# Moving the score-maximum matmuls next to the value matmuls, and normalising queries and keys two token tiles at a time, in a hand-scheduled language-model layer

## The chip, the cores and the metric

The kernel runs on one core of one Trainium2 chip. The metric is the device time of one launch in microseconds, as the median of several runs. The core has five engines that run side by side and meet at semaphores: TensorE (PE in the profile; PEld is its loading of the stationary operand), VectorE (DVE), ScalarE (ACT), GpSimd (POOL) and SyncE (SP), which issues most of the DMA transfers. Each engine takes its own instructions strictly in the order in which the program lists them, and an instruction that waits holds up all that stand behind it on its engine.

## What is computed

`x` holds 2 rows of 2048 token numbers. Each is looked up in an embedding table (50257 entries of width 256), and then one attention layer and one mixture-of-experts layer are added to the residual `h`:

```python
h = take(table, tokens) + bias                     # 2 x 2048 x 256
h = h + attention(layernorm(h))                    # 16 heads of 64, causal
h = h + experts(layernorm(h))                      # top 2 of 8 experts, and a shared one
# attention: xn = layernorm(x) * g + b
q = l2norm(xn @ Wq) * q_scale;  k = l2norm(x @ Wk) * k_scale;  v = x @ Wv   # 2 null keys and values ahead
sim = 8 * q @ k.T - slope * distance;  attn = softmax(causal(sim));  out = (attn @ v) @ Wout
```

The two lines on `q` and `k` are what the change rewrites: each token's 64 numbers per head are divided by their length, and the keys are also multiplied by a vector of 64 scales (`scl` holds `q_scale * k_scale * 8`).

## The kernel before

Two heads are worked on at a time, called a pair: 8 pairs for each of the 2 rows of tokens, 16 pairs `t` in all. The 2048 tokens are 16 tiles of 128 (`T`), and 4 tiles are a group of query columns `ig` (512 wide).

For a pair the work has four stages.

**Projection** (`project`). For each of 17 token tiles `s` PE makes q, k and v of that tile (`proj`, L1400 and L1403). ACT squares q and k (`square`, L875), copies v and copies q and k to `tqk` (L879). DVE sums the squares (`ssq_`, L1083), POOL takes the inverse root with two small instructions (`inv_norm`, L768 and L771), and DVE multiplies (`unit`): one instruction for q (L1094) and one for each of two heads for k (L1096). For every two tiles, a group `g`, ACT and DVE split the result into a high and a low fp16 half in `blk` (`high`, L886; `low_`, L1103), PE transposes them (`turn`, L1415), ACT keeps them (L898) and SP copies parts of them to the tensor `low` (`copy_low`).

**Row maxima** (`maxima`). The softmax subtracts each query's maximum. 44 units per pair (`scores_a`, L1431) are a first, coarser scores matmul for both heads at once: a 64*128 stationary operand in each half of the array. DVE reduces each head's result to a maximum (`max_`, L1123, with a small instruction that reads the result out). The two banks that `scores_a` writes are single: the next `scores_a` waits on PE until both reductions of the one before are done (`a_read`).

**Attention** (`attend`). The keys run down in 44 steps of two blocks (one block of each head; 88 blocks `m` per pair). PE makes the scores (`scores`, L1458 and L1459, on the diagonal also a mask, L1462; stationary operand 128*128), ACT takes the exponential (`exp`, L919) into one of six buffers `probs`, PE multiplies with v (`values`, L1474; stationary operand 128*64, both heads in one pass), and POOL, for one of the eight column groups DVE, adds up the row sums (`sum_p`, L790 and L1161).

**Output**. PE sums over the partitions (`sums`, L1484), ACT copies to `rl`, SP turns the sums by DMA through a column (`turn_l`), DVE inverts (`inv_l`), SP spreads them again by DMA (`spread_l`), DVE divides (`divide`, L1173), PE multiplies with Wout (`wout`, L1494), and DVE adds to `h` (`add_o`, L1181).

At last come the gate and the experts (`gate`, `routed`, `shared_expert`), which the change hardly touches.

All of it is interleaved by a plan written out by hand. `at(time, kind, ...)` gives every piece a due time; the unit of time is one block of `attend`, so that a pair takes 88 units. The plan is sorted, and each engine issues its part of every piece in that order. The due times set an order only; nothing waits for a time. While pair `t` is attended, the projection of pair `t + 1` and its maxima run in between. `turn_of` keeps pieces that use one of the two shared banks a certain distance apart. For a pair that begins at `t0`:

```python
at(t0 + m - 0.9 * (m % 2), "scores", t, m)           # 0, 0.1, 2, 2.1, 4, ...
at(t0 + (m | 1) + 3.5, "values", t, m)               # 4.5, 4.5, 6.5, 6.5, ...
s0 = max(s0 + step, halves[(t, ...)])                # scores_a: from t0 - 35 in steps of 1.85
project(t, t0 + PAIR * t - 74.0, 5.0)                # a token tile every 5 units
```

## Time and profile before

| | us |
|---|---|
| median of 3 runs | 2745.8 (2736.39 to 2750.08) |
| the profiled execution, its own time | 2751.77 |
| its span, first to last instruction | 2750.0 |
| PE busy | 2424.1 (88%) |
| DVE busy | 2027.2 (74%) |
| POOL busy | 1594.1 (58%) |
| ACT busy | 1406.6 (51%) |

Shares of busy time are averages over stages. In the profile, a row of a group gives busy time, the mean duration of one instruction, and the idle time of its engine just before instructions of that group with what ended it. A matmul's duration holds its way through the array; two that follow each other start closer together than one lasts, so the distance between starts in the timeline is the time that one costs PE. `64*128 64x512` is a stationary operand of 64 rows and 128 columns with a moving one of 512 columns. The first pair is attended from 114 us on, the sixteenth pair's last scores stand at 2433 us, and the rest is the experts.

### The profile page before, as it was taken

Reading aid. Unit: us, or ns where it says so; the run is one execution under the profiler, and the core shown is the slowest. Engines: PE = TensorE matmul, PEld = TensorE weight load, DVE = VectorE, ACT = ScalarE, POOL = GpSimd, SP = SyncE. Lnnn points to the kernel's source line nnn. Section 1 sums busy time; section 2 is a strip of 40 time slices with the busy share of each in tenths; the row PEclk is TensorE's granted clock in tenths of the full one; section 3 lists DMA queues with packets and bytes.
Section 4 is the critical chain, followed back from the end, with each engine's and each line's share of the span. In section 5 each row is a group of like instructions: output and inputs, shape, how many; then the busy total and the mean of one; then the engine's idle time right before and its main releaser. Section 6 shows DMA issues by size and latency. Waiting matters only on the chain.

```text
span 2750.0 us, 49117 instructions
## 1 busy us (share of the span) xinstructions
PE 2424.1 (88%) x13353; PEld 1204.6 (44%) x13353; DVE 2027.2 (74%) x5748; ACT 1406.6 (51%) x3094; POOL 1594.1 (58%) x1901
## 2 busy tenths in 40 slices
PE   2789999999989988898999999999999997877887
PEld 2434344444434434343444444444434443446775
DVE  6678787878777878878787878787878786644444
ACT  3445455655554646565555555554646563324541
POOL 6365656666675656575757575656565665462424
PEclk8899999999999999999999999999999998868999
DMA  2000111011111011011111000001000002023543
GB/s 46 18 19 19 34 25 37 24 36 26 30 45 23 24 25 31 20 34 28 34 28 30 17 22 15 25 16 25 16 25 15 21 15 82 9 86 112 163 128 123
DMA packets 155702, 106.65 MB, mean 39 GB/s; under 512 B 63728, under 2 KB 139632, under 8 KB 155440
## 3 DMA queue, kind: packets, MB, share of 16 engines
q1 hardware_dynamic: 147760, 82.52, 11.6%
q0 software_dynamic: 7680, 20.98, 2.5%
q8 instruction: 122, 2.00, 0.3%
q14 instruction: 140, 1.15, 0.2%
HBM read 52.94 MB, written 33.29 MB: 31 GB/s over the span
## 4 chain that ended last, share of the span: by engine, by line
PE 29%; DVE 10%; DMA 6%; issue 5%; POOL 2%; SPq 2%; ACT 2%; another core or an unknown queue 1%; ACTq 0%; DVEq 0%; POOLq 0%
PE ps L1474 5%; PE ps L1458 3%; DVE ps L1123 3%; PE ps L1459 3%; DMA rl<-l_row 3%; PE ps L1555 2%; PE ps L1431 2%; PE ps L1541 2%; PE ps L1403 2%; DMA l_row<-l_col 2%; PE ps L1494 1%; PE ps L1400 1%; DVE acc L1161 1%; DVE tqk L1096 1%; PE ps L1484 1%
## 5 line engine op out<-in xcount | busy, mean ns | idle before, releaser
L790 POOL TENSOR_TENSOR acc<-acc,probs 128x512 f32<-128x512 f32 (+4 forms) x944 | 911.5, 966 | 200.3 <-ACT probs L919 114.8
L919 ACT ACTIVATE probs<-ps,btab 128x512 f32<-128x512 f32 (+4 forms) x1408 | 775.5, 589 | 445.8 <-PE ps L1459 282.8
L1123 DVE CUSTOM_DVE_ANT_0 ps<-ps,tab_l 128x512 f32<-128x512 f32 (+1 forms) x896 | 565.9, 671 | 172.4 <-PE ps L1431 170.3
L1474 PE MATMUL ps<-probs,arena 128*64 128x512 f32 (+4 forms) x2816 | 642.7, 534 | 0.0
L1458 PE MATMUL ps<-arena 128*128 128x512 f16 (+4 forms) x1408 | 482.8, 343 | 23.1 <-ACT probs L919 10.6
L1459 PE MATMUL ps<-arena 128*128 128x512 f16 (+9 forms) x1408 | 479.6, 341 | 0.0
L1431 PE MATMUL ps<-arena 64*128 64x512 f16 (+4 forms) x1408 | 247.2, 344 | 120.1 <-DVE mx L1123 115.3
L768 POOL TENSOR_SCALAR nsq<-ssq 128x4 f32<-128x4 f32 (+1 forms) x272 | 62.0, 228 | 475.3 <-DVE ssq L1083 474.2
L771 POOL TENSOR_TENSOR rnorm<-nsq,minus_half 128x4 f32<-128x4 f32 (+1 forms) x272 | 282.6, 1039 | 22.6
L1403 PE MATMUL ps<-wqkv,xT 128*128 128x256 f32 (+1 forms) x1088 | 287.4, 388 | 0.0
L1431 PEld LDWEIGHTS ps<-arena 64*128 64x128 f16 x1408 | 74.9, 93 | 464.1 <-issue 454.4
L1458 PEld LDWEIGHTS ps<-arena 128*128 128x128 f16 (+1 forms) x1408 | 137.2, 97 | 272.5 <-issue 129.4
L1096 DVE SCALAR_TENSOR_TENSOR tqk<-tqk,rnorm,scl 128x64 f32<-128x64 f32 (+1 forms) x544 | 247.8, 494 | 0.0
L1123 DVE CUSTOM_DVE_ANT_0 ps<-ps,tab_r 128x258 f32<-128x258 f32 (+2 forms) x512 | 207.2, 445 | 51.2 <-PE ps L1431 49.4
L1094 DVE TENSOR_TENSOR tqk<-tqk,rnorm 128x128 f32<-128x128 f32 x256 | 184.9, 722 | 69.4 <-POOL rnorm L771 67.9
L1474 PEld LDWEIGHTS ps<-probs,arena 128*64 128x64 f32 (+1 forms) x2816 | 142.5, 138 | 197.9 <-issue 118.8
L875 ACT ACTIVATE sq<-ps 128x256 f32<-128x256 f32 (+1 forms) x272 | 101.6, 373 | 241.6 <-PE ps L1403 241.6
L886 ACT ACTIVATE blk<-tqk 128x512 f16<-128x512 f32 x128 | 80.7, 630 | 281.0 <-DVE tqk L1096 281.0
L1494 PE MATMUL ps<-wo,otf 128*128 128x256 f32 x512 | 177.2, 429 | 42.6 <-DVE otf L1173 41.0
L1123 DVE DVE_READ_ACCUMULATOR2_ANT mx<- 128x1 f32 x1408 | 194.2, 138 | 0.0
L1403 PEld LDWEIGHTS ps<-wqkv,xT 128*128 128x128 f32 (+1 forms) x1088 | 183.9, 189 | 22.0 <-issue 2.2
L1400 PE MATMUL ps<-wqkv,xnT 128*128 128x128 f32 x1024 | 178.2, 298 | 4.8 <-ACT xnT L865 4.8
(176 smaller groups left out, 3350.5 us busy)
## 6 DMA issues: line engine op xcount, KB each, us to landing
arena<-arena SPq DMA_DIRECT2D x512, 32.0 KB, 1.9
rl<-l_row SPq DMA_DIRECT2D x128, 128.0 KB
x_rows<-arena SPq DMA_DIRECT2D x78, 128.0 KB, 2.2
arena<-x_rows SPq DMA_DIRECT2D x78, 128.0 KB
...
```

The costliest lines, as they stand in the source:

```text
L771: pool.tensor_tensor(rnorm[0:rows, s % 2, c0:4], nsq[0:rows, s % 2, c0:4], minus_half[0:rows, c0:4], ALU.pow).then_inc(rnorm_ready, 1)
L790: pool.tensor_tensor(a, probs[0:rows, (n - 2) % PB, 0:GW] if first else a, p, ALU.add).then_inc(sum_pool, 1)
L919: nc.scalar.activation(probs[0:rows, n % PB, 0:w], bank(S0 + n % 2)[0:rows, 0:w], ACT.Exp, bias=btab[0:rows, hh, z:z + 1]).then_inc(exp_do ...
L1096: last = nc.vector.scalar_tensor_tensor(out=k[:, hd, :], in0=k[:, hd, :], scalar=rnorm[0:rows, s % 2, 2 + hd:3 + hd], in1=scl[0:rows, :], ...
L1123: nc.vector.tensor_tensor_reduce(bank(A0 + hd)[:, 0:w], bank(A0 + hd)[:, 0:w], tab, 1.0, NEG, ALU.add, ALU.max, mx[:, hd, it, c:c + 1]).th ...
L1400: mm(o[:, 0:128], xnT[:, c, 128 * s:128 * s + 128], wqkv[:, r, c, 0:128], start=(c == 0), stop=(c == C - 1))
L1403: last = mm(o[0:rows, 128:384], xT[:, c, 128 * s:128 * s + rows], wqkv[:, r, c, 128:384], start=(c == 0), stop=(c == C - 1))
L1431: mm(bank(A0 + i)[:, 0:w], l[half, 0, i, 128 * it:128 * it + 128], l[half, 1, i, k0:k0 + w], start=True, stop=True).then_inc(a_ready, 1)
L1458: mm(dst[0:rows, 0:w], s[:, 1, hd, j], s[:, 0, hd, q], start=True, stop=False)
L1459: last = mm(dst[0:rows, 0:w], l[SPAN[hd], 1, hd, j], l[SPAN[hd], 0, hd, q], start=False, stop=not diag)
L1474: mm(bank(O0 + o % 2)[DH * hd:DH * hd + DH, c0:GW], vt[t % 2][0:rows, jt, hd, :], probs[0:rows, n % PB, 0:GW - c0], start=(jt == 0), stop= ...
L1494: mm(bank(z)[:, 0:D], otf[:, o % 2, 128 * k:128 * k + 128], wo[:, r, :], start=True, stop=True).then_inc(w_ready, 1)
```

## The change

It has three parts.

1. **The order on PE.** `scores_a` is given due times on a grid: always 1.88 units after an even block, with its steps of 1.92 rounded up to the next place of that grid. `values` is due at 1.95 of the same two units instead of 0.5, so that `scores_a` stands straight ahead of `values`, and `values` straight ahead of the next two blocks of scores. The reduction `max` is due together with its `scores_a`.
2. **Norms and unit vectors for two tiles at once.** `ssq`, `inv_norm` and `unit` run once for a group `g` of two tiles (9 times per pair instead of 17). `ssq` sums 8 rows of 64 (a 128x512 input) and is followed by a new multiplication of the keys with `scl` (128x256), which needs no norm; `unit` is one multiplication of q and k of both tiles with the inverse norms (128x512) in place of six. `sq` has one buffer of 512 instead of two of 256, so that the squares of a new group wait for `ssq` of the group before. `tqk` and `blk` are numbered on through the pairs.
3. **Places in a pair.** The projection starts at 77.5 instead of 74 units ahead of its pair and the maxima at 42 instead of 35. `values`, `sum_p`, `exp` and `sums` have new lags; `divide` is due 9.1 instead of 6.1 units after `sums`, `wout` 11.4 instead of 7.7; the distances of `turn_of`, and the places of the embedding of the second row and of its gate, move too.

The diff, cut to its core:

```diff
-        apart = 0.65 if time < 0 else 0.9
+        apart = 0.7 if time < 0 else 1.05
...
-    LAGS = [dict(square=0.4, ssq=1.2, inv=1.9, unit=3.2, high=3.5, low=4.3, turn=4.8),
-            dict(square=0.9, ssq=2.0, inv=2.3, unit=4.2, high=5.0, low=5.8, turn=7.0)]
+    LAGS = [dict(square=0.3, ssq=1.05, inv=1.6, unit=2.0, high=3.3, low=4.1, turn=5.55),
+            dict(square=1.0, ssq=1.6, inv=2.8, unit=4.2, high=5.0, low=5.5, turn=7.0)]
...
-            s0 = max(s0 + step, halves[(t, (units[n][0] + 1) // 2)])
+            due = max(due + step, halves[(t, (units[n][0] + 1) // 2)])
+
+            s0 = t0 + 2 * math.ceil((due - t0 - 1.88) / 2) + 1.88 if t > 0 else due
             at(s0, "scores_a", t, n)
-            at(s0 + 0.6, "max", t, n)
+            at(s0 + 0.0, "max", t, n)
...
-                s1 = turn_of(s0 + 5.5)
+                s1 = turn_of(s0 + 4.5)
                 at(s1, "turn_shift", t, ig)
...
-            at(t0 + m - 0.9 * (m % 2) + 0.5, "exp", t, m)
-            at(t0 + m - 0.9 * (m % 2) + 1.85, "sum_p", t, m)
-            at(t0 + (m | 1) + 3.5, "values", t, m)
+            at(t0 + m - 0.9 * (m % 2) + 0.8, "exp", t, m)
+            at(t0 + m - 0.9 * (m % 2) + 2.6, "sum_p", t, m)
+            at(t0 + (m | 1) + 2.95, "values", t, m)
...
-            at(s0 + 6.1, "divide", t, ig)
+            at(s0 + 9.1, "divide", t, ig)
...
-                w0 = turn_of(max(sums_at[(t, ig)] + 7.7, wout_from[0] + 2.4))
+                w0 = turn_of(max(sums_at[(t, ig)] + 11.4, wout_from[0] + 2.4))
...
-    project(0, -24, 1.7)
-    maxima(0, -14.4, 1.2)
+    project(0, -24, 1.25)
+    maxima(0, -14.4, 1.3)
...
-        project(t, t0 + PAIR * t - 74.0, 5.0)
+        project(t, t0 + PAIR * t - 77.5, 5.0)
     for t in range(1, PAIRS):
-        maxima(t, t0 + PAIR * t - 35.0, 1.85)
+        maxima(t, t0 + PAIR * t - 42.0, 1.92)
...
-                need(act, ssq_ready, n - 1)
-                nc.scalar.activation(sq[0:rows, s % 2, c0:256], p[0:rows, c0:256], ACT.Square).then_inc(sq_ready, 1)
+                need(act, ssq_ready, PG * t + s // 2)
+                nc.scalar.activation(sq[0:rows, :].rearrange("p (z u n) -> p z u n", z=2, u=2)[:, c0 // 128:2, s % 2, :],
+                                     p[0:rows, c0:256].rearrange("p (z n) -> p z n", n=128), ACT.Square).then_inc(sq_ready, 1)
...
+                dve.wait_ge(sq_ready, done)
                 need(dve, nsq_ready, n - 1)
-                nc.vector.tensor_reduce(ssq[0:rows, s % 2, c0:4], sq[0:rows, s % 2, 64 * c0:256].rearrange("p (a d) -> p a d", d=DH),
+                nc.vector.tensor_reduce(ssq[0:rows, (PG * t + g) % 2, cs], sq[0:rows, DH * cs.start:DH * cs.stop].rearrange("p (a d) -> p a d", d=DH),
                                         AX.X, ALU.add).then_inc(ssq_ready, 1)
...
+                k = tqk[0:rows, (PG * t + g) % 2, 256:DH * cs.stop].rearrange("p (a d) -> p a d", d=DH)
+                dve.wait_ge(p_read, done)
+                nc.vector.tensor_tensor(k, k, scl[0:rows, :].unsqueeze(1).to_broadcast([rows, cs.stop - 4, DH]), ALU.mult).then_inc(k_scaled, 1)
...
-                if s < T:
-                    nc.vector.tensor_tensor(q, q, rnorm[0:rows, s % 2, 0:2].unsqueeze(2).to_broadcast([rows, 2, DH]), ALU.mult)
-                for hd in range(2):
-                    last = nc.vector.scalar_tensor_tensor(out=k[:, hd, :], in0=k[:, hd, :], scalar=rnorm[0:rows, s % 2, 2 + hd:3 + hd],
-                                                          in1=scl[0:rows, :], op0=ALU.mult, op1=ALU.mult)
-                last.then_inc(qk_read, 1)
+                dve.wait_ge(k_scaled, n + 1)
+                qk = tqk[0:rows, (PG * t + g) % 2, DH * cs.start:DH * cs.stop].rearrange("p (a d) -> p a d", d=DH)
+                nc.vector.tensor_tensor(qk, qk, rnorm[0:rows, (PG * t + g) % 2, cs].unsqueeze(2).to_broadcast([rows, cs.stop - cs.start, DH]),
+                                        ALU.mult).then_inc(qk_read, 1)
```

The order of PE in the middle of a pair before, rows in a row. L1458 and L1459 are the scores (`arena` holds their operands), L1474 is `values`, L1431 `scores_a`, L1494 `wout`, L1400 and L1403 a projection:

```order
L1474 MATMUL ps<-probs,arena 64x512 x2
L1400 MATMUL ps<-wqkv,xnT 128x128 x2
L1403 MATMUL ps<-wqkv,xT 128x256 x2
L1431 MATMUL ps<-arena 128x512 x2
L1494 MATMUL ps<-wo,otf 128x256
L1458 MATMUL ps<-arena 128x512
L1459 MATMUL ps<-arena 128x512
L1458 MATMUL ps<-arena 128x512
L1459 MATMUL ps<-arena 128x512
L1474 MATMUL ps<-probs,arena 64x512 x2
L1431 MATMUL ps<-arena 128x512 x2
L1458 MATMUL ps<-arena 128x512
```

The order of PE in the change near the same place of a pair; its lines stand 5 further down (L1463 and L1464 scores, L1479 `values`, L1436 `scores_a`, L1499 `wout`, L1405 and L1408 a projection):

```order
L1479 MATMUL ps<-probs,arena 64x512 x2
L1463 MATMUL ps<-arena 128x512
L1464 MATMUL ps<-arena 128x512
L1463 MATMUL ps<-arena 128x512
L1464 MATMUL ps<-arena 128x512
L1405 MATMUL ps<-wqkv,xnT 128x128 x2
L1408 MATMUL ps<-wqkv,xT 128x256 x2
L1436 MATMUL ps<-arena 128x258 x2
L1479 MATMUL ps<-probs,arena 64x512 x2
L1463 MATMUL ps<-arena 128x512
```

`scores_a` no longer stands alone among 128*128 operands; it is followed by `values`. Counted over the whole program, PE changes from one size of the stationary operand to another 2718 times before and 2559 times after, and the number of `scores_a` (704) that have neither `values` nor `sums` for a neighbour falls from 212 to 58.

The order of PE in the change further on in the same pair, among the diagonal blocks (L1467 is the mask):

```order
L1463 MATMUL ps<-arena 128x258
L1464 MATMUL ps<-arena 128x258
L1467 MATMUL ps<-mask_b,ident 128x128
L1436 MATMUL ps<-arena 128x258 x2
L1436 MATMUL ps<-arena 128x386 x2
L1479 MATMUL ps<-probs,arena 64x386 x2
```

Two `scores_a` fall on one place of the grid and follow each other directly, with nothing between them. This happens 28 times in pairs 2 to 15; before, no two stood side by side there.

The order of DVE in the middle of a pair before. L1123 is `max` (shown as ISA, with its read-out), L1173 `divide`, L1083 `ssq`, L1094 and L1096 `unit`:

```order
L1083 TENSOR_REDUCE ssq<-sq 128x4
L1173 TENSOR_TENSOR otf<-ps,rl 128x512
L1123 ISA ps,mx<-ps,tab_l 128x512
L1123 ISA mx 128x1
L1123 ISA ps,mx<-ps,tab_l 128x512
L1123 ISA mx 128x1
L1094 TENSOR_TENSOR tqk<-tqk,rnorm 128x128
L1096 SCALAR_TENSOR_TENSOR tqk<-tqk,rnorm,scl 128x64 x2
```

The order of DVE in the change at a like place (L1128 `max`, L1178 `divide`, L1090 and L1094 `ssq` and the scaling of the keys, L1102 `unit`, L1186 `add_o`):

```order
L1090 TENSOR_REDUCE ssq<-sq 128x8
L1094 TENSOR_TENSOR tqk<-tqk,scl 128x256
L1186 TENSOR_TENSOR h<-ps,h 128x256
L1128 ISA ps,mx<-ps,tab_l 128x256
L1128 ISA mx 128x1
L1128 ISA ps,mx<-ps,tab_l 128x256
L1128 ISA mx 128x1
L1178 TENSOR_TENSOR otf<-ps,rl 128x512
L1102 TENSOR_TENSOR tqk<-tqk,rnorm 128x512
```

Three wide instructions (L1090, L1094, L1102) stand for a group of two tiles, where eight stood before (L1083, L1094 and twice L1096 for each tile).

## Rows read from the trace of the kernel before

**Rows 1.** The windows view: us, busy us (instructions) of PE, PEld, DVE, ACT, POOL, PEclk.

```profile
268.00:2270.00 2002.00, 1846.91 (x10289) 833.34 (x10286) 1592.20 (x4447) 1109.53 (x2429) 1237.16 (x1450) 0.97 0.11 26
0.00:114.00 114.00, 52.94 (x253) 38.29 (x254) 71.75 (x227) 42.00 (x113) 60.78 (x111) 0.84 0.15 35
```

**Rows 2.** Waits of PE alone, 268 to 2270 us: us in total, times, longest.

```profile
PE ps L1431 <- DVE mx L1123: 84.1, 152, 2.2
PE ps L1494 <- DVE otf L1173: 35.9, 27, 2.8
PE ps L1458 <- ACT probs L919: 10.2, 14, 0.8
PE ps L1458 <- DMA arena<-augs: 6.7, 13, 1.2
PE ps L1415 <- DVE blk L1103: 6.5, 16, 1.8
```

**Rows 3.** Timeline of PE, 1300 to 1326 us: start, length, instruction, idle before it.

```profile
1308.95 0.38 PE L1458 MATMUL ps<-arena 128*128 128x512 f16 x1
1309.17 0.38 PE L1459 MATMUL ps<-arena 128*128 128x512 f16 x1
...
1310.62 0.39 PE L1431 MATMUL ps<-arena 64*128 64x512 f16 x2
1310.94 0.71 PE L1400 MATMUL ps<-wqkv,xnT 128*128 128x128 f32 x4
...
1323.38 1.08 PE L1474 MATMUL ps<-probs,arena 128*64 128x512 f32 x4
1324.39 0.23 PE L1458 MATMUL ps<-arena 128*128 128x130 f16 x1
...
1324.58 0.66 PE L1400 MATMUL ps<-wqkv,xnT 128*128 128x128 f32 x4
```

**Rows 4.** Groups of DVE by shape: busy us, mean ns | idle before, and its end.

```profile
L1123 DVE CUSTOM_DVE_ANT_0 ps<-ps,tab_l 128x512 f32<-128x512 f32 x768 | 514.7, 710 | 168.4 <-PE ps L1431 166.9
L1096 DVE SCALAR_TENSOR_TENSOR tqk<-tqk,rnorm,scl 128x64 f32<-128x64 f32 x512 | 240.4, 508 | 0.0
...
L1094 DVE TENSOR_TENSOR tqk<-tqk,rnorm 128x128 f32<-128x128 f32 x256 | 184.9, 722 | 69.4 <-POOL rnorm L771 67.9
...
L1103 DVE TENSOR_TENSOR blk<-tqk,blk 128x512 f16<-128x512 f32 x128 | 117.5, 918 | 3.2 <-ACT blk L886 3.2
...
L1123 DVE CUSTOM_DVE_ANT_0 ps<-ps,tab_r 128x258 f32<-128x258 f32 x256 | 103.9, 447 | 35.9 <-PE ps L1431 35.9
L1083 DVE TENSOR_REDUCE ssq<-sq 128x4 f32<-128x256 f32 x256 | 103.7, 405 | 7.2 <-ACT sq L875 7.2
```

**Rows 5.** Single lines of DVE: shortest/median/longest ns.

```profile
L1094 DVE TENSOR_TENSOR tqk<-tqk,rnorm x256: 271/590/1406, 50.7 to 2277.8; 128x128 f32<-128x128 f32 x128
...
L1103 DVE TENSOR_TENSOR blk<-tqk,blk x128: 633/749/1675, 65.7 to 2292.9; 128x512 f16<-128x512 f32 x128
```

**Rows 6.** Groups of POOL by shape.

```profile
L771 POOL TENSOR_TENSOR rnorm<-nsq,minus_half 128x4 f32<-128x4 f32 x256 | 271.4, 1060 | 21.3
...
L768 POOL TENSOR_SCALAR nsq<-ssq 128x4 f32<-128x4 f32 x256 | 58.6, 229 | 460.3 <-DVE ssq L1083 459.3
...
L762 POOL TENSOR_TENSOR rstd<-var,minus_half 128x2 f32<-128x2 f32 x48 | 36.6, 763 | 4.0
```

**Rows 7.** Waits of DVE in the whole span: us in total, times, longest.

```profile
DVE otf L1173 <- DMA rl<-l_row: 104.5, 48, 4.3
DVE tqk L1094 <- POOL rnorm L771: 67.9, 62, 4.0
```

**Rows 8.** Timeline of PE, one `scores_a`.

```profile
1334.26 0.39 PE L1431 MATMUL ps<-arena 64*128 64x512 f16 x2
```

**Rows 9.** Timeline of DVE, its second reduction and the read-out.

```profile
1335.30 0.73 DVE L1123 CUSTOM_DVE_ANT_0 ps<-ps,tab_l 128x512 f32<-128x512 f32 x1
1335.95 0.14 DVE L1123 DVE_READ_ACCUMULATOR2_ANT mx<- 128x1 f32 x1
```

More of the change, by code:

```diff
@@ L1 @@
+import math
 import concourse.bass as bass
@@ L140, in project @@
             at(s0 + lag["square"], "square", t, s)
-            at(s0 + lag["ssq"], "ssq", t, s)
-            at(s0 + lag["inv"], "inv_norm", t, s)
-            at(s0 + lag["unit"], "unit", t, s)
             if s == 0:
@@ L147, in project @@
                 g = s // 2
+                at(s0 + lag["ssq"], "ssq", t, g)
+                at(s0 + lag["inv"], "inv_norm", t, g)
+                at(s0 + lag["unit"], "unit", t, g)
                 at(s0 + lag["high"], "high", t, g)
@@ L363, in lm_tower_kernel @@
         rstd = sb("rstd", [128, 3, NB, T])
-        minus_half = sb("minus_half", [128, 4])
+        minus_half = sb("minus_half", [128, 8])
         wqkv = sb("wqkv", [128, 2, C, 3 * 128])
         wo = sb("wo", [128, 2, D])
-        sq = sb("sq", [128, 2, 256])
-        ssq = sb("ssq", [128, 2, 4])
-        nsq = sb("nsq", [128, 2, 4])
-        rnorm = sb("rnorm", [128, 2, 4])
+        sq = sb("sq", [128, 512])
+        ssq = sb("ssq", [128, 2, 8])
+        nsq = sb("nsq", [128, 2, 8])
+        rnorm = sb("rnorm", [128, 2, 8])
         tqk = sb("tqk", [128, 2, 512])
@@ L762, in root, with inv_norm @@
                 pool.tensor_tensor(rstd[:, k, b, us], var[:, k, b, us], minus_half[:, 0:2], ALU.pow).then_inc(rstd_ready[k], 1)
-            def inv_norm(t, s):
-                n = TK * t + s
-                rows, c0 = (128, 0) if s < T else (NN, 2)
+            def inv_norm(t, g):
+                n = PG * t + g
+                rows, cs = (128, slice(0, 8)) if g < PG - 1 else (NN, slice(4, 6))
                 pool.wait_ge(ssq_ready, n + 1)
-                pool.tensor_scalar(nsq[0:rows, s % 2, c0:4], ssq[0:rows, s % 2, c0:4], 1e-24, None, ALU.max).then_inc(nsq_ready, 1)
+                pool.tensor_scalar(nsq[0:rows, (PG * t + g) % 2, cs], ssq[0:rows, (PG * t + g) % 2, cs], 1e-24, None, ALU.max).then_inc(nsq_ready, 1)
                 pool.wait_ge(nsq_ready, n + 1)
                 need(pool, qk_read, n - 1)
-                pool.tensor_tensor(rnorm[0:rows, s % 2, c0:4], nsq[0:rows, s % 2, c0:4], minus_half[0:rows, c0:4], ALU.pow).then_inc(rnorm_ready, 1)
+                pool.tensor_tensor(rnorm[0:rows, (PG * t + g) % 2, cs], nsq[0:rows, (PG * t + g) % 2, cs], minus_half[0:rows, cs], ALU.pow).then_inc(rnorm_ready, 1)
             def sum_p(t, m):
```

80 lines of the change are left out of this document (39 added, 41 removed).

## The prediction

> **What bounds the kernel now.** I read the windows view first. Between 268 and 2270 us, 14 of the 16 pairs, PE is busy 1847 of 2002 us at a granted clock of 0.97, DVE 1592, POOL 1237, ACT 1110 [rows 1]. PE sets the pace, about 143 us a pair, and there are two ways to be faster: less time of PE itself, and less of the 155 us that it idles there. The waits of PE say what the idle time is [rows 2]: 84 us are `scores_a` waiting for the reductions of the one before, 36 us are `wout` waiting for `divide`, and three waits of 6 to 10 us each are scores behind an exponential, scores behind the DMA of the maxima, and the transposes behind `low_`. The clock is near its upper level (2.4 GHz) here, so it has little to give.
>
> **The change, part by part**, against the profiled execution's 2751.8 us; the median of the runs is 6 us below that.
>
> *Changes of the stationary size.* Two scores matmuls of 512 columns start 0.22 us apart; `scores_a`, also 512 columns, is followed by the projection's 128*128 operand after 0.32 us [rows 3]. So a change from one size to another costs PE 0.10 us. 159 fewer of them (2718 to 2559 by the order) are 159 x 0.10 = **-15 us**. It is small because half of the `scores_a` already had a neighbour of values before. Ends: 10 and 20 us less.
>
> *Wout.* It moves from 7.7 to 11.4 units behind `sums`, 3.7 units or some 6 us at 143 / 88 = 1.6 us a unit, and `divide` 3 units. The longest of its waits was 2.8 us [rows 2]. All 36 us should go: **-36**, ends -42 and -25. What is late next is the write to `h`, for which nobody waits within a pair.
>
> *The DMA of the maxima.* The maxima begin 7 units earlier, but step 1.92 instead of 1.85 over 43 steps gives 3 back; the last ones come 4 units earlier, over 6 us, against waits of 1.2 us: **-7**.
>
> *The grid for scores_a.* The banks of `scores_a` come free only after both reductions. From its start at 1334.26 [rows 8] to the end of the second read-out at 1336.09 [rows 9] there are 1.83 us at 512 columns; at 258 columns each reduction is 710 - 447 = 0.26 us shorter [rows 4], so 1.30 us. Where two `scores_a` follow each other directly, the first being 258 wide and 0.2 us long each time, PE must stand for 1.1 us: 28 x 1.1 = +31. Also, in each pair there are three places on the diagonal with nothing but `values` and narrow scores between two `scores_a`. The widest has values of 1.01 us and scores of 0.19 us a block [rows 3] with more columns; by such rows they take 1.7, 1.5 and 1.3 us, which is 0.1 + 0.3 + 0.5 short of 1.83: 14 pairs x 1 = +14. Together **+45**, ends +25 (where DVE would have been late anyway) and +55.
>
> *Norms of two tiles at once, on DVE.* Before, two tiles cost 2 x 0.405 (L1083) + 2 x 0.722 (L1094) + 4 x 0.508 (L1096) = 4.29 us [rows 4]. No row shows the new shapes. The shortest L1094 took 0.271 us for 128 elements and the shortest L1103 0.633 for 512 [rows 5], so 256 elements take about 0.39 at best. Over their shortest, L1094 lost on average 722 - 271 = 0.45 us and L1103 918 - 633 = 0.29 [rows 4, 5]: the loss is one per instruction and doesn't grow with width. So I take 0.39 + 0.3 for the scaling of k, 0.92 for `unit` (as L1103), and 0.405 + 0.26 for the reduction over 512 (a reduction's slope by the 258 and 512 rows, [rows 4]): 2.28 us. 128 groups x 2.0 us = 257 us less on DVE, 13% of its 2027. If the loss grew with width instead, as from 0.45 at 128 elements to 0.9 and 1.8, the three would cost 4.4 us and nothing would be saved. The mean of L1103 speaks against that. The Trainium skill (SBUF — State Buffer, "SBUF: two separate sides") says that DVE instructions with two inputs in SBUF and GpSimd instructions take one port pair by turns, each for its whole length, and whoever comes second waits; by that a delay is paid per meeting, the rows agree, and the sum stays with the per-instruction price. By the same rule wider DVE instructions hold GpSimd off for longer at a time, though for less in all.
>
> DVE is not on PE's path by its sum but by its order: what stands ahead of a reduction makes it late. There are 257 us less of that, and the waits that stood ahead of reductions, 104.5 us of `divide` for its DMA and 67.9 us of `unit` for POOL [rows 7], are due 3 units later and once instead of twice a group. `max` is also due together with its `scores_a`. Of the 84 us of lateness I take seven tenths away: **-60**, ends 0 and -84.
>
> *POOL.* Two tiles cost 2 x (0.229 + 1.060) = 2.58 us. The power takes 0.763 for 2 elements and 1.060 for 4 [rows 6], 0.15 each, so 1.65 for 8, with 0.23 ahead: 1.88 us, 0.7 less per group, 89 us in all. POOL isn't waited for by ACT to speak of, so: 0. But the answer to one `ssq` now comes 0.6 us later, and a `sum_p` may stand ahead; if that cover goes, `unit` waits (rival C).
>
> *ACT, SP.* The instructions of ACT are the same in number and size, and those of SP too; SP's queue passes the same DMAs, `turn_l` earlier and the parts of `low` at the pace of the projection. The squares have one buffer, and ACT waits for `ssq` of the last group, due 3 units before the next tile: 0. The small waits for exponential and transposes, 10.2 + 6.5 us [rows 2], have less in front: **-10**, ends 0 and -17.
>
> *First pair and tail.* Until 114 us PE is busy 53 us and DVE 72 [rows 1]; there the projection is on the path, and 8 groups x 2 us of DVE go, of which I count half: **-8**, ends 0 and -16. The tail keeps its work: 0.
>
> Sum: -15 - 36 - 7 + 45 - 60 - 10 - 8 = -91, or 2751.8 - 91 = 2661 on the profiled execution and **2655** as a median.
>
> **The rivals.**
>
> *A, the stalls go altogether.* If all 84 us of lateness, the small waits and the upper half of the startup go, and the direct neighbours overlap with lateness that was there anyway (+25), the sum is -20 - 42 - 7 + 25 - 84 - 17 - 16 = -161: 2585. For it: DVE has only 1592 of 2002 us to do now. Against it: the 28 neighbours can't be hidden in the order itself.
>
> *B, DVE isn't relieved*, because the wide instructions lose more per instruction than the narrow ones or meet POOL each time; lateness stays and the waits only change place: -15 - 36 - 7 + 45 = -13 to, with a third of the lateness gone and the small terms, -30: 2725. For it: new shapes have no row. Against it: L1103 and L1094 as above.
>
> *C, slower: `unit` waits for POOL ahead of the reductions.* The plan gives `unit` 1.4 units (2.3 us) after `inv_norm`, of which the power now takes 1.88. One `sum_p` in front (over 1 us) makes DVE stand, and the reduction behind it, `scores_a`, `values` and the next scores, which now stand behind each other on PE, stand too. It already waited 67.9 us in 62 cases [rows 7]. If each of 128 groups held PE for 0.5 us, with no lateness removed, and `wout` gained as forecast, the sum is -15 - 36 - 7 + 45 + 64 = +51: 2797. It decides from 0.1 us a group on if nothing else is gained. Against it: 89 us less on POOL, and half as many such waits.
>
> *D, the change isn't in effect on the chip.* The order shows the pieces moved; it could only be that 0.10 us for a change of size is hidden elsewhere. That is 15 us and within the range.
>
> **How the numbers follow.** The forecast has 0.55, A 0.17, B 0.18, C 0.10. The range leaves out C and the part of A below 2570: 2570 to 2735, and takes in the ends of lateness in both directions. A measurement of this kernel can tell about 0.5% (14 us) from no change. Faster by more: the forecast, A, and over half of B, 0.82; within: the rest of B, 0.08; slower: C, 0.10.
>
> **What would show it.** PE's waits in the same 14 pairs: `wout` on `divide` near 0 (else the Wout step is wrong); `scores_a` on `max` 45 + 24 = 70 us, of which 28 waits of about 1.1 us; if over 130, DVE was not relieved. DVE's three new groups at 0.67, 0.69 and 0.92 us in the mean and a busy time of about 1770 us; B if the two multiplications together are over 2.5 us. POOL's power at 1.65 us. C would show as `unit` waiting over 130 us for `rnorm`. A pair should take 137 us instead of 143. Wrong above all: a wait for the exponential or for POOL's sums in place of those for DVE.

## The result, and the profile after

The change takes 2636.0 us as a median of 4 runs (2633.92 to 2640.77), the kernel before in the same comparison 2747.9 us (2736.39 to 2750.51): a ratio of 0.9603, 95% interval [0.9572, 0.9634]. The forecast was 2655, range 2570 to 2735.

The profiled execution of the change. First the page: span, busy time of each engine, and of the 40 slices the rows of PE, DVE and the granted clock:

```profile
span 2633.1 us, 47837 instructions
PE 2370.3 (90%) x13353; PEld 1210.4 (46%) x13353; DVE 1816.8 (69%) x5108; ACT 1419.1 (54%) x3094; POOL 1558.9 (59%) x1645
PE   3789999999999999899999999999999998867897
DVE  6668686767776788768686868686868686634445
PEclk9799999999999999899999999999999998868999
```

The windows view: the same 14 pairs as in [rows 1] (columns as there), then the start and the experts:

```profile
259.00:2160.00 1901.00, 1802.53 (x10285) 840.47 (x10283) 1395.10 (x3885) 1121.38 (x2428) 1206.13 (x1224) 0.98 0.12 27
0.00:119.00 119.00, 56.98 (x294) 41.60 (x295) 77.46 (x222) 47.77 (x127) 62.05 (x103) 0.90 0.15 35
2309.00:2633.00 324.00, 255.70 (x1418) 211.30 (x1416) 144.43 (x396) 115.10 (x258) 124.61 (x131) 0.88 0.41 127
```

From here on the stretch of the 14 pairs goes from the first scores of pair 2 to the first of pair 16, to the tenth of a us. Of the 117 us between the spans (2750.0 and 2633.1), 100 lie in it (2001.5 to 1901.1 us), 13 in the last pair (163 to 149.5), 10 in the start with the first pair, and the experts give 7 back (317 to 324). PE is busy for 95% of the stretch, where it was 92% in [rows 1].

The waits of PE in the stretch, as [rows 2]. `wout` for `divide` was second there and is gone, and so are the scores' waits for the exponential and for the DMA of the maxima:

```profile
PE ps L1436 <- DVE mx L1128: 75.0, 84, 3.5
PE ps L1391 <- issue: 7.1, 2, 3.7
PE ps L1499 <- ACT tqk L884: 5.2, 13, 0.4
PE ps L1443 <- ACT arena L903: 4.8, 13, 0.4
```

The waits of DVE in the stretch, as [rows 7]. `divide` waits for its DMA 1.6 us instead of 91.5 (in the whole span 2.4 instead of 104.5); new is one wait of up to 5.4 us per pair for the squares. The first row is the kernel before in its stretch, the others are the change:

```profile
DVE otf L1173 <- DMA rl<-l_row: 91.5, 41, 4.3
```

```profile
DVE ssq L1090 <- ACT sq L879: 70.5, 13, 5.4
DVE tqk L1102 <- POOL rnorm L775: 32.7, 69, 1.7
...
DVE otf L1178 <- DMA rl<-l_row: 1.6, 3, 1.0
```

The groups of DVE and of POOL by shape, which answer to [rows 4] and [rows 6]:

```profile
L1102 DVE TENSOR_TENSOR tqk<-tqk,rnorm 128x512 f32<-128x512 f32 x128 | 155.4, 1214 | 44.2 <-POOL rnorm L775 44.1
...
L1108 DVE TENSOR_TENSOR blk<-tqk,blk 128x512 f16<-128x512 f32 x128 | 126.5, 988 | 2.5 <-ACT blk L891 2.4
...
L1090 DVE TENSOR_REDUCE ssq<-sq 128x8 f32<-128x512 f32 x128 | 86.4, 675 | 70.7 <-ACT sq L879 70.7
...
L1094 DVE TENSOR_TENSOR tqk<-tqk,scl 128x256 f32<-128x256 f32 x128 | 58.8, 459 | 0.0
```

```profile
L775 POOL TENSOR_TENSOR rnorm<-nsq,minus_half 128x8 f32<-128x8 f32 x128 | 214.5, 1676 | 10.7
```

The three wide instructions together take 0.675 + 0.459 + 1.214 = 2.35 us a group, where eight took 4.29 by their mean durations.

**A measure for what follows.**
| run | stretch | PE idle | at the lower level | stretch - idle - half of that |
|---|---|---|---|---|
| before | 2001.5 | 155.1 | 102.4 | 1795 |
| the change | 1901.1 | 98.5 | 81.9 | 1762 |
| e4_out_late | 1916.0 | 103.6 | 30.7 | 1797 |
| f_norms_out | 1928.1 | 110.0 | 41.0 | 1798 |
| e1_norms | 1954.5 | 121.1 | 78.5 | 1794 |
| e2_places | 1937.1 | 117.7 | 105.8 | 1766 |
| e3_no_grid | 1930.5 | 105.3 | 58.0 | 1796 |
| e6_one_each | 1946.9 | 138.0 | 109.2 | 1754 |
| c2_one_each_early | 1983.2 | 164.9 | 119.5 | 1759 |
| e8_split_unit | 1975.4 | 142.9 | 136.5 | 1764 |
| e10_max_early | 2058.8 | 197.1 | 153.6 | 1785 |
| e7_apart | 2098.9 | 219.4 | 194.6 | 1782 |
| e5_out_early | 2087.3 | 249.7 | 215.0 | 1730 |

So the change took 57 us out of idling, 10 out of the clock and 34 out of PE's own work. The last column is no pure number: idling and the lower level overlap (most in e5_out_early), and it also takes in what the trace doesn't mark as idle. If the lower level is counted only while PE is busy, the column becomes 1764 for the change and for no run with its grid over 1771, e5_out_early included (1765), except e10_max_early (1787); the kernel before and the four runs without the grid have 1797 to 1799, and e7_apart 1795.

### The profile page after: what moved, and what is told of

Its sections match the earlier page's. It is cut to its first block, busy times and chain, and to the rows that moved or that the text cites. A ratio compares the mean times of both kernels' runs of the same rounds, so it can differ in the third digit from the quotient of the medians.

```text
span 2633.1 us, 47837 instructions
## 1 busy us (share of the span) xinstructions
PE 2370.3 (90%) x13353; PEld 1210.4 (46%) x13353; DVE 1816.8 (69%) x5108; ACT 1419.1 (54%) x3094; POOL 1558.9 (59%) x1645
## 3 DMA queue, kind: packets, MB, share of 16 engines
q14 instruction: 130, 1.06, 0.1%
## 4 chain that ended last, share of the span: by engine, by line
PE 68%; DVE 11%; POOL 9%; issue 7%; ACT 1%; DMA 1%; another core or an unknown queue 1%; SPq 1%; POOLq 0%; ACTq 0%; DVEq 0%
PE ps L1479 17%; PE ps L1463 9%; PE ps L1408 8%; PE ps L1464 7%; PE ps L1436 7%; POOL acc L794 5%; PE ps L1405 4%; DVE ps L1128 4%; PE ps L1499 4%; PE ps L1489 2%; PE ps L1560 2%; PE ps L1546 2%; PE ps L1420 2%; POOL rnorm L775 2%; DVE tqk L1102 1%
## 5 line engine op out<-in xcount | busy, mean ns | idle before, releaser
L794 POOL TENSOR_TENSOR acc<-acc,probs 128x512 f32<-128x512 f32 (+4 forms) x944 | 934.6, 990 | 326.7 <-ACT probs L924 240.6
L924 ACT ACTIVATE probs<-ps,btab 128x512 f32<-128x512 f32 (+4 forms) x1408 | 759.2, 587 | 649.9 <-PE ps L1464 367.0
L1128 DVE CUSTOM_DVE_ANT_0 ps<-ps,tab_l 128x512 f32<-128x512 f32 (+1 forms) x896 | 567.5, 674 | 324.5 <-PE ps L1436 321.9
L1479 PE MATMUL ps<-probs,arena 128*64 128x512 f32 (+4 forms) x2816 | 637.1, 528 | 0.2 <-DVE otf L1178 0.2
L1463 PE MATMUL ps<-arena 128*128 128x512 f16 (+4 forms) x1408 | 476.6, 340 | 0.3 <-DMA arena<-augs 0.3
L1464 PE MATMUL ps<-arena 128*128 128x512 f16 (+9 forms) x1408 | 471.6, 337 | 0.0
L1463 PEld LDWEIGHTS ps<-arena 128*128 128x128 f16 (+1 forms) x1408 | 135.5, 96 | 507.2 <-issue 336.6
L1436 PE MATMUL ps<-arena 64*128 64x512 f16 (+4 forms) x1408 | 245.0, 342 | 99.8 <-DVE mx L1128 95.9
L1408 PE MATMUL ps<-wqkv,xT 128*128 128x256 f32 (+1 forms) x1088 | 297.2, 398 | 0.1
L1128 DVE CUSTOM_DVE_ANT_0 ps<-ps,tab_r 128x258 f32<-128x258 f32 (+2 forms) x512 | 208.4, 448 | 97.2 <-PE ps L1436 94.0
L775 POOL TENSOR_TENSOR rnorm<-nsq,minus_half 128x8 f32<-128x8 f32 x144 | 226.0, 1570 | 12.0
L772 POOL TENSOR_SCALAR nsq<-ssq 128x8 f32<-128x8 f32 x144 | 47.8, 332 | 309.8 <-DVE ssq L1090 308.0
L1436 PEld LDWEIGHTS ps<-arena 64*128 64x128 f16 x1408 | 72.9, 93 | 342.9 <-issue 328.3
L1479 PEld LDWEIGHTS ps<-probs,arena 128*64 128x64 f32 (+1 forms) x2816 | 142.2, 135 | 137.4 <-issue 84.1
L1408 PEld LDWEIGHTS ps<-wqkv,xT 128*128 128x128 f32 (+1 forms) x1088 | 190.5, 196 | 22.0 <-issue 0.3
L1128 DVE DVE_READ_ACCUMULATOR2_ANT mx<- 128x1 f32 x1408 | 197.1, 140 | 0.0
L1102 DVE TENSOR_TENSOR tqk<-tqk,rnorm 128x512 f32<-128x512 f32 x144 | 162.9, 1131 | 44.4 <-POOL rnorm L775 44.2
L1499 PE MATMUL ps<-wo,otf 128*128 128x256 f32 x512 | 171.0, 416 | 13.9 <-ACT tqk L884 7.2
L1405 PE MATMUL ps<-wqkv,xnT 128*128 128x128 f32 x1024 | 174.7, 296 | 9.3 <-ACT xnT L869 5.5
L794 POOL TENSOR_TENSOR acc<-probs 128x512 f32<-128x512 f32 x80 | 105.4, 1318 | 118.6 <-ACT probs L924 113.4
L1405 PEld LDWEIGHTS ps<-wqkv,xnT 128*128 128x128 f32 x1024 | 152.9, 202 | 33.8 <-issue 7.8
```

The costliest lines, as they stand in the source:

```text
L775: pool.tensor_tensor(rnorm[0:rows, (PG * t + g) % 2, cs], nsq[0:rows, (PG * t + g) % 2, cs], minus_half[0:rows, cs], ALU.pow).then_inc(rno ...
L794: pool.tensor_tensor(a, probs[0:rows, (n - 2) % PB, 0:GW] if first else a, p, ALU.add).then_inc(sum_pool, 1)
L924: nc.scalar.activation(probs[0:rows, n % PB, 0:w], bank(S0 + n % 2)[0:rows, 0:w], ACT.Exp, bias=btab[0:rows, hh, z:z + 1]).then_inc(exp_do ...
L1102: nc.vector.tensor_tensor(qk, qk, rnorm[0:rows, (PG * t + g) % 2, cs].unsqueeze(2).to_broadcast([rows, cs.stop - cs.start, DH]), ALU.mult) ...
L1128: nc.vector.tensor_tensor_reduce(bank(A0 + hd)[:, 0:w], bank(A0 + hd)[:, 0:w], tab, 1.0, NEG, ALU.add, ALU.max, mx[:, hd, it, c:c + 1]).th ...
L1405: mm(o[:, 0:128], xnT[:, c, 128 * s:128 * s + 128], wqkv[:, r, c, 0:128], start=(c == 0), stop=(c == C - 1))
```

## The experiments

All ratios are to the kernel before, run on the same chip, with 95% intervals. The kernel before itself took 2699 to 2748 us on the chips of these runs, so times are compared only through the ratio or inside the stretch.

**The parts alone.** e1_norms is the kernel before with only the two-tile norms:

```diff
-            at(s0 + lag["ssq"], "ssq", t, s)
-            at(s0 + lag["inv"], "inv_norm", t, s)
-            at(s0 + lag["unit"], "unit", t, s)
...
                 g = s // 2
+                at(s0 + lag["ssq"], "ssq", t, g)
+                at(s0 + lag["inv"], "inv_norm", t, g)
+                at(s0 + lag["unit"], "unit", t, g)
```

> The kernel before with the two-tile norms alone: ssq, inv_norm and unit once per two tiles, all due times as before. Theory 1 (DVE's time ahead of the reductions was a large part of PE's idle time): the 84 us that scores_a waits for max in 14 pairs fall to 30 or less, wout's wait for divide stays near 36, time 2685 to 2700. Theory 2 (the order was what mattered, DVE's work was hidden): within 15 us of before, 2733 to 2750, with DVE's busy time 200 us lower all the same.

Measured: 2661.7 us, 0.9857 [0.9834, 0.988]. DVE's busy time fell to 1842.5 us, `scores_a` waits 67.6 us for reductions instead of 84.1, and `wout` 13.9 instead of 35.9, probably since `divide` itself now has less in front of it. Neither theory had this: the lateness of the reductions hardly fell, and the time did.

e2_places is the other half, the change's plan with norms and unit vectors tile by tile as before:

```diff
-                at(s0 + lag["ssq"], "ssq", t, g)
-                at(s0 + lag["inv"], "inv_norm", t, g)
-                at(s0 + lag["unit"], "unit", t, g)
+            at(s0 + lag["ssq"], "ssq", t, s)
+            at(s0 + lag["inv"], "inv_norm", t, s)
+            at(s0 + lag["unit"], "unit", t, s)
```

> The changed kernel's plan (grid, lags, places in a pair) with the norms per tile as before; the buffers of tqk, blk and the norms are numbered on through the pairs, which the plan needs. Theory 1: changes of size -15, wout -36, maxima's DMA -7, against +45 at the grid, and DVE late as before: 2725 to 2745. Theory 2: most of the gain is here, 2660 or less. If both parts are independent, the gains of this run and of the norms alone add up to 112 us; if they need each other, they add up to well under it.

Measured: 2642.8 us, 0.9795 [0.9771, 0.982]; `scores_a` waits 89.7 us for reductions. That is between the two theories. The two halves add up to 3.5% against 4.0% for the whole: nearly additive. Half of the gain needs no wide instruction.

**`divide` and `wout` later, and nothing else:**

```diff
-            at(s0 + 6.1, "divide", t, ig)
+            at(s0 + 9.1, "divide", t, ig)
...
-                w0 = turn_of(max(sums_at[(t, ig)] + 7.7, wout_from[0] + 2.4))
+                w0 = turn_of(max(sums_at[(t, ig)] + 11.4, wout_from[0] + 2.4))
```

> The kernel before with divide and wout alone at the new distances behind sums (9.1 and 11.4). The prediction's step: wout's wait goes, 36 us, ratio 0.985 to 0.989. If the wait of divide for its DMA also makes reductions late there, as putting it back into the changed kernel did (8% slower): 60 us or more, ratio under 0.978, and scores_a's wait of 84 us falls too.

Measured: 2659.2 us, 0.9732 [0.9701, 0.9763]: two numbers of the plan give 2.7%, the largest single piece. Windows view and waits of PE of this run:

```profile
269.00:2185.00 1916.00, 1812.39 (x10286) 828.60 (x10284) 1601.94 (x4445) 1105.91 (x2428) 1242.09 (x1449) 0.99 0.11 27
```

```profile
PE ps L1431 <- DVE mx L1123: 76.9, 137, 2.8
PE ps L1458 <- ACT probs L919: 10.4, 14, 0.8
PE ps L1415 <- DVE blk L1103: 6.2, 17, 1.8
```

The wait of `wout` is gone (36 us). The stretch is 85 us shorter, though: 51 of idling and, by the table, 36 because the clock stands at its lower level for 31 us instead of 102. In the trace of the kernel before, the granted clock falls 20 times in the stretch, and in 15 of them PE has just stood at `wout`, for 0.9 to 2.5 us; in this run it falls 8 times, never behind a stand of `wout`. DVE is as busy as before (1602 against 1592 us in [rows 1]), and that cost nothing.

The same edit undone in the change:

```diff
-            at(s0 + 9.1, "divide", t, ig)
+            at(s0 + 6.1, "divide", t, ig)
...
-                w0 = turn_of(max(sums_at[(t, ig)] + 11.4, wout_from[0] + 2.4))
+                w0 = turn_of(max(sums_at[(t, ig)] + 7.7, wout_from[0] + 2.4))
```

> The changed kernel with divide and wout at their old distances behind sums (6.1 and 7.7). The prediction gave the move 36 us: then this is 30 to 40 us slower than the changed kernel, with wout waiting for divide 30 us and divide for its DMA about 100 us again. If DVE, relieved by the two-tile norms, hides it: under 15 us slower.

Measured: 2808.2 us, 1.0415 [1.0376, 1.0455], slower than the kernel before and far outside both expectations. In the stretch `divide` waits 207 us for its DMA (56 times; 91.5 us before the change) and `scores_a` 225 us for reductions (135 times). One case, first on DVE, then on PE (start, length, instruction, idle before it and its end):

```profile
1480.49 0.47 DVE L1128 CUSTOM_DVE_ANT_0 ps<-ps,tab_l 128x256 f32<-128x256 f32 x1
...
1486.22 0.69 DVE L1178 TENSOR_TENSOR otf<-ps,rl 128x512 f32<-128x512 f32 x1 [5.21 <-DMA rl<-l_row]
...
1487.03 0.42 DVE L1128 CUSTOM_DVE_ANT_0 ps<-ps,tab_r 128x258 f32<-128x258 f32 x1
```

```profile
1481.15 0.29 PE L1436 MATMUL ps<-arena 64*128 64x258 f16 x2
1488.03 0.61 PE L1436 MATMUL ps<-arena 64*128 64x512 f16 x2 [6.59 <-DVE mx L1128]
...
1489.20 0.61 PE L1463 MATMUL ps<-arena 128*128 128x512 f16 x1
1489.60 0.63 PE L1464 MATMUL ps<-arena 65*128 65x512 f16 x1
```

DVE stands at `divide`, the reductions for which PE waits stand behind it, and PE stands for longer than DVE. Then the scores start 0.40 us apart, where at the upper level it was 0.22 [rows 3]: the clock has fallen. The chain is `divide` -> reduction -> `scores_a` -> clock. In the changed plan this place of `divide` is far worse than in the old one. Why is not shown; each `scores_a` now has `values` and two blocks of scores straight behind it, which would do it.

**Do the norms add to that?** f_norms_out has e1_norms and e4_out_late together:

```diff
-            at(s0 + lag["ssq"], "ssq", t, s)
...
+                at(s0 + lag["ssq"], "ssq", t, g)
...
-            at(s0 + 6.1, "divide", t, ig)
+            at(s0 + 9.1, "divide", t, ig)
```

> The kernel before with two parts of the change and nothing else: norms of two tiles at once, and divide and wout at 9.1 and 11.4 behind sums. PE's order by size and the grid stay out: 2701 changes of size against 2559 in the changed kernel. Apart, the two parts gave 0.9857 and 0.9732. If they are independent of each other and of the grid: 0.957 to 0.962, the whole of the change, and the grid brings nothing beyond its 16 us of size changes that its own stalls eat up. If both parts took the same lateness away: 0.967 to 0.973, and the grid is what the rest of the gain comes from.

Measured: 2636.9 us, 0.9754 [0.9731, 0.9777], against 0.9732 [0.9701, 0.9763] without the norms: nothing on top, and less than either theory said. DVE has 163 us less to do in the stretch, and `scores_a` still waits 73.1 us (133 times). The freed time shows as stands of DVE itself: 285 us for `scores_a` where e4_out_late has 186, and 72 us for the transposed maxima where it has 6. Work taken off DVE went into waits that its order holds; which piece then makes `scores_a` late isn't shown. In the changed plan the same norms are worth 1.9% (from e2_places, 0.9795, to the change).

**The grid.** Its rounding taken away:

```diff
-            s0 = t0 + 2 * math.ceil((due - t0 - 1.88) / 2) + 1.88 if t > 0 else due
+            s0 = due
```

> The changed kernel with scores_a due where its steps of 1.92 put it, not on the grid: 2773 changes of stationary size instead of 2559 and 4 directly following scores_a instead of 34. If a change of size costs 0.10 us and a direct neighbour 1.1 us: +21 - 31, so 2625 to 2645, no difference. If the grid's even rhythm is itself worth something (DVE is given each reduction at equal distances): slower, 2660 to 2690, with more waits of scores_a for max.

Measured: 2623.7 us, 0.9716 [0.9693, 0.9739]; the grid is worth 1.1%, 29 us in the stretch, where the forecast's own prices made it no difference. PE's waits without it:

```profile
PE ps L1436 <- DVE mx L1128: 29.5, 42, 3.0
PE ps L1463 <- ACT probs L924: 20.9, 41, 2.8
PE ps L1420 <- DVE blk L1108: 12.0, 14, 0.9
```

So the grid brings 75.0 - 29.5 = 45 us of waiting for reductions, as forecast, but PE's other waits fall by about 50 (from 72 to 22 us), and its idle time as a whole is 7 us less with the grid, against which it stands 24 us longer at the lower level. PE's own work is 34 us less. The order has 2773 changes of size without the grid and 2559 with it, 214 x 0.10 = 21 us of these.

The same rhythm, but `scores_a` between the two blocks and not ahead of `values`:

```diff
-            s0 = t0 + 2 * math.ceil((due - t0 - 1.88) / 2) + 1.88 if t > 0 else due
+            s0 = t0 + 2 * math.ceil((due - t0 - 1.0) / 2) + 1.0 if t > 0 else due
```

> The changed kernel with the grid at 1.0 of two units instead of 1.88: the same rhythm and the same 34 direct neighbours, but scores_a stands in the middle among 128*128 operands; 2677 changes of size instead of 2559. Price of the change of size alone: 118 x 0.10 = +12, 2648. If the place straight ahead of values matters for other reasons (the reductions are in time only there), 2670 or more; if values and the next scores are held up by scores_a's wait, faster than 2636.

Measured: 2804.0 us, 1.0378 [1.035, 1.0407]. 118 more changes of size are 12 us; the stretch is 198 us longer. `scores_a` waits 146.8 us. PE's own work, with the lower level counted only while PE is busy, is 31 us more. Since the reductions move with their `scores_a` also on DVE, this run doesn't tell PE's order from DVE's. So the next one leaves PE's order untouched and moves `max` alone, on DVE:

```diff
-            at(s0 + 0.0, "max", t, n)
+            at(s0 - (0.88 if t > 0 else 0.0), "max", t, n)
```

> The changed kernel with PE's order untouched and the reductions due 0.88 units earlier in DVE's order, where the run with the grid at 1.0 had them. DVE then stands waiting at a reduction whose scores_a has not run, with other work behind it. If the large loss of the grid at 1.0 (1.038 against before, 0.96 for the change) comes from the place on DVE: at least half of it here too, ratio to before over 0.99. If it comes from the place on PE: within 1% of the changed kernel.

Measured: 2762.6 us, 1.0235 [1.0192, 1.0278]. PE's waits in its 14 pairs:

```profile
PE ps L1436 <- DVE mx L1128: 48.1, 69, 2.4
PE ps L1489 <- POOL acc L794: 40.8, 27, 1.7
PE ps L1420 <- DVE blk L1108: 31.2, 42, 0.9
PE ps L1463 <- ACT probs L924: 22.6, 41, 1.7
```

The reductions now come early enough (48.1 instead of 75.0 us), but DVE stands 535 us in front of them for PE instead of 371, and what stands behind is late: `low_` for the transposes, its own share of the row sums, `unit`, and through them POOL and ACT. With no instruction of PE moved this costs 158 us in the stretch. The 28 direct neighbours wait 1.04 to 1.12 us each here. In the same run PE's own work seems 23 us longer with the same order. It has 250 stands of PE in the stretch, the change 118: what a stand costs may not all be marked as idle (23 us on 132 stands would be 0.17 us each). So of the 34 us of the grid no more than the 21 of the changes of size are shown.

**One `scores_a` at each place.** With a step of 2.0 no two meet:

```diff
-        maxima(t, t0 + PAIR * t - 42.0, 1.92)
+        maxima(t, t0 + PAIR * t - 42.0, 2.0)
```

> The changed kernel with maxima in steps of 2.0 instead of 1.92, so that each place of the grid holds one scores_a: 4 direct neighbours (all in the first pair) instead of 34, with the same number of changes of size within 4. If the 28 direct neighbours cost PE 1.1 us each, as the prediction counted: 31 us less than the changed kernel, ratio to it 0.988. If they only overlap with lateness that is there anyway, or the last maxima now come too late for the scores of their group: within 5 us or slower.

Measured: 2645.1 us, 0.9797 [0.9768, 0.9827], worse than the change. The target was met: `scores_a` waits 32.8 us instead of 75.0. But once per pair ACT and PE look like this:

```profile
464.50 0.72 ACT L941 ACTIVATE tab_l<-pos,slopes 128x512 bf16<-128x512 f16 x1 [5.57 <-DVE aug L1140]
465.13 0.80 ACT L942 ACTIVATE tab_r<-pos,back,slopes 128x514 bf16<-128x514 f16 x1
...
468.05 1.24 ACT L924 ACTIVATE probs<-ps,btab 128x512 f32<-128x512 f32 x2
```

```profile
462.77 1.08 PE L1479 MATMUL ps<-probs,arena 128*64 128x512 f32 x4
468.77 0.50 PE L1463 MATMUL ps<-arena 128*128 128x386 f16 x1 [4.93 <-ACT probs L924]
```

The maxima of a pair now end later, after the place where `tables` (L941 to L944) for the next pair stands on ACT. It must wait for them, and the exponentials stand behind it. The scores wait 70.6 us in 14 cases.

Both earlier, maxima and tables:

```diff
-        maxima(t, t0 + PAIR * t - 42.0, 1.92)
+        maxima(t, t0 + PAIR * t - 45.5, 2.0)
...
-            at(t0 + PAIR * t - 45.0 if t else -16, "tables", t)
+            at(t0 + PAIR * t - 48.5 if t else -16, "tables", t)
```

> The changed kernel with one scores_a per place of the grid (maxima in steps of 2.0), and, unlike the run with steps of 2.0 alone, begun 45.5 instead of 42 units ahead so that the last maxima stand at the same block (41) as in the changed kernel; the tables are made 3.5 units earlier too. Theory: the run with steps of 2.0 alone took away the stall of direct neighbours (starts of scores_a to scores_a 59.6 to 2.4 us) and lost 85 us where scores wait for the late maxima. Without that wait: 30 to 57 us faster than the changed kernel, ratio to before 0.941 to 0.951. Rival: the even rhythm at 2.0 itself, which gives the free places back to full ones, is what cost: ratio 0.97 or more.

Measured: 2717.4 us, 0.9949 [0.9928, 0.9969], so the hoped-for gain is out. I moved the tables by as much as the maxima, so that they stood ahead of the last `scores_a` again: the same wait, 70.8 us in 14 cases, and more behind it. The ratio fits the expectation's rival, the even rhythm of 2.0 itself, but doesn't show it, since the wait for the tables stayed. Whether two neighbours a pair can be saved with the tables left in place wasn't tried; the change with its 28 pairs of neighbours is the best that was run.

**Width against number of instructions.** `unit` as two instructions of 256 elements:

```diff
-                nc.vector.tensor_tensor(qk, qk, rnorm[0:rows, (PG * t + g) % 2, cs].unsqueeze(2).to_broadcast([rows, cs.stop - cs.start, DH]),
-                                        ALU.mult).then_inc(qk_read, 1)
+                parts = [slice(0, 4), slice(4, 8)] if g < PG - 1 else [cs]
+                for part in parts:
...
+                    last = nc.vector.tensor_tensor(qk, qk, rnorm[0:rows, (PG * t + g) % 2, part].unsqueeze(2).to_broadcast([rows, part.stop - part.start, DH]),
+                                                   ALU.mult)
+                last.then_inc(qk_read, 1)
```

> The changed kernel with unit as two multiplications of 256 elements (q, then k) instead of one of 512, 128 instructions more on DVE. The one of 512 takes 1.21 us in the mean against 0.67 at its shortest. If the loss is one per instruction, as the prediction took it: each of the two 0.41 + 0.5, together 1.8 us, 75 us more on DVE and 10 to 40 us slower. If the loss comes from what POOL runs when unit is released, once: the first loses 0.5 and the second nearly nothing, together 1.35 us, and the time stays within 10 us of the changed kernel.

Measured: 2711.9 us, 0.9919 [0.9891, 0.9946]. Its group on DVE:

```profile
L1104 DVE TENSOR_TENSOR tqk<-tqk,rnorm 128x256 f32<-128x256 f32 x256 | 244.2, 993 | 43.9 <-POOL rnorm L775 43.9
```

Two halves take 2 x 0.993 = 1.99 us, the whole 1.21. A half takes 0.402 at its shortest, so it loses 0.59 us, and the whole in the change 0.669, so it loses 0.55: the loss is one per instruction, whatever the width. It isn't paid once a group either: the first halves take 0.96 us in the mean, the second ones 1.03. And it goes with POOL. In the change the 118 wide `unit` that start while POOL is busy take 1.26 us in the mean, the other 10 take 0.69; of the halves 235 take 1.04 and 21 take 0.42. The Trainium skill (SBUF — State Buffer, "SBUF: two separate sides") lets GpSimd and a DVE instruction with two inputs in SBUF have the shared port pair by turns, each for its whole length; these durations agree. `unit` keeps DVE busy for 89 us more (155.4 to 244.2), DVE as a whole 65 (1816.8 to 1882.2). The stretch is 74 us longer, more than the 10 to 40 expected, with `scores_a` waiting 106.8 us: in this plan DVE's time reaches PE, though DVE is idle for a quarter of it.

**The change once more**, on another chip:

> The changed kernel itself, unchanged, as the measure for the other runs of this chip, since absolute times differ from chip to chip (before took 2748 us on one and 2700 on another). Every theory: ratio to before 0.957 to 0.963.

Measured: 2595.7 us, 0.9618 [0.959, 0.9646]; the stretch is 1901.8 us, as on the first chip (1901.1). The experts take 290 us on this chip and 324 on the other.

## Why the prediction was right, and where not

*Wout, -36.* Right in its mechanism, under half of its size. The idle time of 36 us went to 0, as e4_out_late shows for this edit alone, but its stretch fell by 85: 51 of idling, the rest above all the clock. What failed is the sentence that the clock "has little to give": a mean of 0.97 hid 102 us at the lower level, 51 us of cost, and in 15 of 20 cases PE fell there just behind a stand at `wout` of 0.9 to 2.5 us. The change shows the same where a stand is left. `scores_a` twice in a row, and what follows, then the same two projections further on:

```profile
1298.52 0.29 PE L1436 MATMUL ps<-arena 64*128 64x258 f16 x2
1301.17 0.34 PE L1436 MATMUL ps<-arena 64*128 64x386 f16 x2 [2.36 <-DVE mx L1128]
...
1302.71 1.17 PE L1405 MATMUL ps<-wqkv,xnT 128*128 128x128 f32 x4
1303.67 1.91 PE L1408 MATMUL ps<-wqkv,xT 128*128 128x256 f32 x4
...
1309.91 0.61 PE L1405 MATMUL ps<-wqkv,xnT 128*128 128x128 f32 x4
1310.36 1.03 PE L1408 MATMUL ps<-wqkv,xT 128*128 128x256 f32 x4
```

About 1.5 us behind the stand the projection costs 0.96 us to the next start, against 0.45 further on. The Trainium skill (TensorE: Matmul & The Clock Gate, "What's actually happening") says that the clock follows how busy PE has been; these rows agree.

*The grid, +45.* The stalls were right in sum and wrong in make. Grid on against grid off, waits for reductions are 45 us more. But the 28 direct neighbours, taken at 1.1 us, cost about 1.8 us each, some 50 us, and the diagonal next to nothing. That mean is of two kinds: 14 neighbours, one a pair, wait 1.04 to 1.06 us, as in the first row below, and the other 14 wait 2.2 to 3.5. So 1.1 us holds where DVE is free. At the neighbours further up it wasn't, as the rows of DVE show:

```profile
1238.78 0.39 PE L1436 MATMUL ps<-arena 64*128 64x512 f16 x2 [1.04 <-DVE mx L1128]
```

```profile
1295.60 0.69 DVE L1090 TENSOR_REDUCE ssq<-sq 128x8 f32<-128x512 f32 x1 [5.38 <-ACT sq L879]
...
1298.88 1.35 DVE L1102 TENSOR_TENSOR tqk<-tqk,rnorm 128x512 f32<-128x512 f32 x1 [0.52 <-POOL rnorm L775]
1300.16 0.42 DVE L1128 CUSTOM_DVE_ANT_0 ps<-ps,tab_r 128x258 f32<-128x258 f32 x1
```

DVE has stood 5.38 us for the squares, once a pair, which the forecast's 0 for ACT didn't have, and `unit` stands ahead of the reduction, waits for POOL and takes 1.35 us. This is rival C in small. Not forecast either was that the grid takes about 50 us off other waits.

*DVE's lateness, -60.* `scores_a` waits for reductions 75.0 us; the forecast said 70, of which 45 new, and here it is about 50 of neighbours and 25 of others. So the old lateness fell by 59 us, as said. Why is another matter: 257 us less of DVE was the argument, and with `divide` late the norms alone gave nothing (f_norms_out). It is the places and the norms together (e2_places has 89.7, e1_norms 67.6, the change 75.0 with the neighbours in).

*Changes of size, -15.* The price stands as the rows gave it, but no run confirms it: PE's own work fell by 34 us in the stretch, and only 14 of them are the 144 fewer changes there at 0.10. The other 20 I can't assign, and e3_no_grid has 56 changes more than the kernel before in the stretch and the same own work (1796 against 1795). Part may be stands, 242 before and 118 in the change, whose cost isn't all marked as idle; but f_norms_out has 182 and the same 1798. The forecast's reason, that half of the `scores_a` already stood next to `values`, was loose: 460 of 704 did.

*DMA of the maxima, -7, small waits, -10.* Both gone as said; in their place stand 17 us of other small ones (the `issue` wait, `wout` and `turn_shift` behind ACT). The wait for the DMA of the maxima is gone in e4_out_late too, which leaves the maxima where they were, so their earlier start isn't shown to be what removed it. *First pair, -8:* 10 measured, by luck. The start, which was to gain, got 5 us longer (113.5 to 118.6 us up to the first scores), and the first pair's attention 15 shorter (155 to 140). With the norms alone (e1_norms) the start gained 2 us. *Tail, 0:* 7 us more in the experts on this chip.

*Norms.* Three groups at 0.675, 0.459 and 1.214 us against 0.67, 0.69 and 0.92 forecast, 2.35 against 2.28 together. `unit` loses 0.55, not 0.3: that was taken from L1103, which itself now takes 0.988 instead of 0.918. POOL's power took 1.676 against 1.65. DVE's busy time was to fall by 257 us to about 1770; it fell by 210 to 1816.8. Of the gap of 47 us, 20 lie in what the old instructions were worth: 4.29 us a group adds up mean durations, but the L1096 overlap, 512 x 0.508 = 260 us of duration in 240.4 us of busy time [rows 4]. Another 9 are the three new groups, and 9 the longer L1103.

*The sum.* In the stretch the terms made -68 of idling (-36 - 7 + 45 - 60 - 10), -15 of PE's work and nothing of the clock, together -83; measured are -57, -34 and -10, together -100. The last pair gave 13 more, which no term had. Rival A is out, since 75 us of lateness stayed; B and C are out by `scores_a` at 75.0 us and `unit` waiting 44.2. That the sum is so near is partly luck: the largest piece, `wout` with its clock, was too small by 49, and the norms on DVE and the late `divide` don't add up as the sum has them.

What stays open: the 20 us of PE's own work; which part of e7_apart's loss is PE's order (e10_max_early, with the place on DVE alone, loses 158 of its 198 us); whether some neighbours could go without the stand of `tables`; and what the other lags and distances of the plan are worth, which no run changed alone.
